# The start of an AdaLN block reordered between its engines, values in fours for two more half periods, and h of the second batch loaded in halves

## The chip, the cores and the metric

One core of a Trainium2 chip. The metric is the device time of one execution in microseconds, the median of several runs. The profiled execution is a single one of them; its times are counted from the start of its span.

## What is computed

A transformer block with adaptive layer norm, for two batches of 1024 rows of 1024 (fp32). Cut to what matters:

```python
mod = (silu(c) @ wmod).reshape(2, 6, 1, 1024)         # shift and scale a, gate a, shift and scale b, gate b
h = layernorm(x) * (1 + ca) + sa
q, k, v = h @ wq, h @ wk, h @ wv                      # 32 heads of 32; q and k are rotated (rope)
a = softmax(causal(q k^T / sqrt(32))) v
x = x + ga * (a @ wo)
h = layernorm(x) * (1 + cb) + sb
x = x + gb * ffn(h)     # h @ W_base^T + b_base, plus 8 gated low-rank experts (A_w, B_w, W_gate, W_thr)
```

## The kernel before

Every fp32 product is made as three products of rounded parts: hi*hi, lo*hi, hi*lo. ScalarE rounds a tile to its hi part, VectorE or GpSimd subtract for the rest (lo). Each engine runs an instruction order written out by hand; semaphores join them. All waits of SyncE's list, which issues nearly all DMAs, are in order too: an issue that waits holds up those behind it.

**The start.** Eight tiles of x (128 rows each) of batch 0 are loaded, normalised on VectorE (`ln_stats`, `ln_norm`; the root is GpSimd's `ln_rstd`), transposed on TensorE (`ln_turn`) and copied to xT (`ln_out`, half on VectorE, half on ScalarE). In the loop of VectorE, tile i-1 is normalised behind the statistics of tile i. wmod comes in 12 chunks of 2 MiB through four buffers; `mod_chunk(k)` multiplies chunk k on TensorE, `mod_out(k)` copies it out on ScalarE, `mod_cols(k)` turns it to columns. After chunk 3 `mod_vectors(0)` gives scale_a and shift_a. Then `ln_mod(c, kt)` scales the 128x512 piece (column block c, chunk kt) of xT on VectorE, `ln_round` rounds it on ScalarE, `ln_rest` subtracts, even kt on VectorE, odd kt on GpSimd. `chain(t, n, m0, m1)` is the projection of head group t: 24 products of 512 columns, n = 0 to 3 for q and k in both column blocks, 4 and 5 for v. Chains (0,0) and (0,2) follow the pieces one by one. Each q or k chain goes through rope: `rope_products` (VectorE), `rope_total` (GpSimd), `round_rot` (ScalarE), `rest_rot` (GpSimd, rot_lo), each waiting for the one before it through one buffer; when rot_lo is 2, then 4, SyncE copies the parts to stk (`stack`). `split_qk`/`rest_qk` and `split_v`/`rest_v` part the weights. `first_rows` then runs the first score rows, with the last wmod chunks and the chains of FIRST_CHAINS between them; wmod's chunks 8 to 11 are issued around the two stacks.

**The half periods.** 32 half periods u (PAIRS), each for two heads and 12 units i of scores; u = 2t and 2t+1 belong to head group t, and batch 1 begins with t = 8. In each unit TensorE has scores, row products for the next half period, a quarter of a chain and values. `PV_AT` sets after which units values are made: every second one, in FOURS every fourth, with six probs buffers instead of four; the last of FOURS has one group more, at unit 10. The two more buffers are x_next and h_pair, which also take wo's rows 0 and 1 at the end. Meanwhile batch 1's h is made and stored to HBM; at u = 13 `load_next_hT(c)` brings it into hT_lo (SyncE's queue) and hT_hi (ScalarE's queue) over batch 0's, block by block, once the last chain that reads the block is done.

**The end of it.** In u = 28 wo is loaded (`load_wo`), in 29 and 30 GpSimd parts it (`split_wo`), and `project` multiplies with it. a_raw and ga lie over buffers of the first phase. **Phase B** goes over 16 tiles; per tile TensorE multiplies h2 (made in two halves: `modulate_half` on VectorE, `split_h` on ScalarE and GpSimd) with wb. Its body waits for both halves, and for y_ev, VectorE's copy of the tile before out of ps_s.

## Time and profile before

| | |
|---|---|
| median of three runs | 1649.58 us (1647.54 to 1650.38) |
| the profiled execution | 1646.6 us, its span 1644.5 us |
| busy: TensorE, VectorE, ScalarE, GpSimd | 1569.2 (95%), 964.9 (59%), 1024.1 (62%), 616.9 (38%) us |
| mean granted TensorE clock | 0.98 of full |
| share of the chain that ended last | TensorE 79%, VectorE 6%, ScalarE 5%, DMA 4% |
| first scores (end of the start) | 138.23 us |

A busy share near 100% says that an engine has no room; the few per cent that are left stand in a few places, which only the timelines show. The granted clock of 1.0 is 2.4 GHz and 0.5 is 1.2 GHz. A line of a timeline can hold several like instructions (x4).

### The profile page before, as it was taken

The numbers are of one execution on the slowest core, as the hardware profiler recorded it, in microseconds if no ns is written. First come the engines' busy times: TensorE is split into PE (matmuls) and PEld (weight loads), VectorE is DVE, ScalarE is ACT, GpSimd is POOL, SyncE is SP. The second block draws the span as 40 slices with busy tenths as digits, with TensorE's granted clock in tenths as the row PEclk, the third lists the DMA queues.
The fourth block names the chain that finished last, engine by engine and source line by source line (L and its number), as shares of the span: only waits on it lengthen the run. The fifth ranks groups of instructions, "written<-read, shape, count | busy, mean of one in ns | idle before, by whom it ended". The sixth has DMA issues, their size and how long they took to land.

```text
span 1644.5 us, 29435 instructions
## 1 busy us (share of the span) xinstructions
PE 1569.2 (95%) x9530; PEld 1187.6 (72%) x9530; DVE 964.9 (59%) x2932; ACT 1024.1 (62%) x2662; POOL 616.9 (38%) x485
## 2 busy tenths in 40 slices
PE   5889999999999989999999999998989999999996
PEld 2556767667677767777777777775668888888885
DVE  5627577677765756566657567565653535353533
ACT  2337888989889978899899899888520101010100
POOL 3533253443534424234234244237114343333332
PEclk9999999999999999999999999996989999999998
DMA  9673444445443384333333333354332121212110
GB/s 350 229 256 82 108 99 126 110 110 146 113 123 79 81 270 98 76 92 77 92 80 87 91 75 82 86 156 135 84 98 72 43 76 39 77 40 77 38 64 26
DMA packets 172035, 174.43 MB, mean 106 GB/s; under 512 B 21045, under 2 KB 120677, under 8 KB 171897
## 3 DMA queue, kind: packets, MB, share of 16 engines
q1 hardware_dynamic: 169784, 168.54, 36.5%
q10 hardware_dynamic: 2112, 4.19, 0.8%
q8 instruction: 68, 1.11, 0.3%
q14 instruction: 71, 0.57, 0.1%
HBM read 96.65 MB, written 25.18 MB: 74 GB/s over the span
## 4 chain that ended last, share of the span: by engine, by line
PE 79%; DVE 6%; ACT 5%; issue 4%; DMA 4%; POOL 1%; SPq 1%; ACTq 0%; DVEq 0%
PE ps_s L1272 13%; PE ps_qkv L1272 13%; PE ps_s L719 11%; PE ps_pv L1341 9%; PE ps_s L1314 8%; PE ps_t L1283 7%; PE ps_qkv L691 5%; PE ps_s L691 5%; PE ps_s L721 1%; ACT probsT L1568 1%; ACT rows_sb L1532 1%; DMA x_start<-in_L_attn_x_dram 1%; DVE rows_sb L1799 1%; PE ps_s L1185 1%; PE ps_t L704 1%
## 5 line engine op out<-in xcount | busy, mean ns | idle before, releaser
L1532 ACT ACTIVATE rows_sb<-rows_sb,bias_m 128x640 f32<-128x640 f32 (+7 forms) x512 | 396.1, 774 | 12.5
L1799 DVE CUSTOM_DVE_ANT_0 rows_sb<-ps_t,mask 128x512 f32<-128x512 f32 (+3 forms) x512 | 296.8, 586 | 168.9 <-PE ps_t L1283 156.4
L1283 PE MATMUL ps_t<-stk 96*128 96x512 f32 (+3 forms) x768 | 268.9, 352 | 10.5 <-DVE smax L1799 7.0
L1568 ACT ACTIVATE probsT<-ps_s 128x512 f32<-128x512 f32 (+1 forms) x504 | 251.8, 537 | 33.6 <-PE ps_s L1314 17.2
L1314 PE MATMUL ps_s<-stk 98*128 98x512 f32 (+3 forms) x768 | 224.8, 374 | 3.2 <-DMA stk<-m_rows 2.0
L1825 DVE TENSOR_TENSOR ps_s<-ps_s,mask_t 128x128 f32<-128x128 f32 (+1 forms) x384 | 120.5, 340 | 158.8 <-PE ps_s L1314 155.5
L1283 PEld LDWEIGHTS ps_t<-stk 96*128 96x128 f32 x768 | 146.5, 191 | 58.8 <-DVE smax L1799 12.2
L1314 PEld LDWEIGHTS ps_s<-stk 98*128 98x128 f32 x768 | 132.4, 192 | 71.8 <-issue 34.3
L1960 POOL TENSOR_TENSOR rope_b<-rope_b,rope_sin 128x512 f32<-128x512 f32 x64 | 82.9, 1295 | 263.0 <-DVE rope_b L1784 263.0
L1272 PE MATMUL ps_qkv<-hT_hi,w_hi 128*128 128x512 f32 x384 | 158.6, 413 | 7.8 <-DVE hT_lo L1759 3.8
L1799 DVE CUSTOM_DVE_ANT_0 rows_sb<-ps_t,mask,smax_part 128x128 f32<-128x128 f32 (+3 forms) x256 | 140.7, 550 | 41.5 <-PE ps_t L1283 13.9
L1936 POOL TENSOR_TENSOR w_lo<-w_raw,w_hi 128x512 fp32r<-128x512 f32 x64 | 84.2, 1318 | 206.4 <-ACT w_hi L1480 206.4
L764 ACT ACTIVATE gsm<-ag_out,bthr 128x1 f32<-128x1 f32 x16 | 4.7, 294 | 248.2 <-DVE ag_out L851 248.2
L1272 PE MATMUL ps_s<-hT_hi,w_hi 128*128 128x512 f32 x384 | 155.9, 406 | 1.6 <-DVE rope_b L1784 1.5
L1272 PE MATMUL ps_qkv<-hT_lo,w_hi 128*128 128x512 f32 x384 | 152.3, 397 | 0.0
L1272 PE MATMUL ps_qkv<-hT_hi,w_lo 128*128 128x512 f32 x384 | 152.2, 396 | 0.0
L1272 PE MATMUL ps_s<-hT_lo,w_hi 128*128 128x512 f32 x384 | 151.4, 394 | 0.0
L1272 PE MATMUL ps_s<-hT_hi,w_lo 128*128 128x512 f32 x384 | 151.0, 393 | 0.0
L1341 PE MATMUL ps_pv<-probsT,v_all 128*32 128x128 f32 (+1 forms) x2272 | 146.0, 348 | 0.0
L1968 POOL TENSOR_TENSOR rot<-rope_b,rot 128x512 fp32r<-128x512 f32 x64 | 84.6, 1321 | 97.4 <-ACT rot L1502 97.4
L719 PE MATMUL ps_s<-wb_hi,h_hi 128*128 128x512 f32 x256 | 109.1, 426 | 7.1 <-POOL h_lo L922 5.1
L1341 PEld LDWEIGHTS ps_pv<-probsT,v_all 128*32 128x32 f32 x2272 | 70.8, 111 | 58.9 <-issue 23.9
(219 smaller groups left out, 3174.6 us busy)
## 6 DMA issues: line engine op xcount, KB each, us to landing
stk<-rot SPq DMA_DIRECT2D x384, 128.0 KB, 2.4
probsT<-in_L_wmod_dram SPq DMA_DIRECT2D x5, 2048.0 KB, 10.3
wm_one<-in_L_wmod_dram SPq DMA_DIRECT2D x5, 2048.0 KB, 14.2
w_raw<-in_L_attn_wq_dram SPq DMA_DIRECT2D x16, 512.0 KB, 4.0
w_raw<-in_L_attn_wk_dram SPq DMA_DIRECT2D x16, 512.0 KB, 4.7
w_raw<-in_L_attn_wv_dram SPq DMA_DIRECT2D x16, 512.0 KB, 4.1
attn_scratch<-attn_sb SPq DMA_DIRECT2D x128, 64.0 KB, 2.8
h_scratch<-h_pair SPq DMA_DIRECT2D x32, 256.0 KB, 2.9
```

The source lines that it names most:

```text
L691: mm = pe.matmul(q_bank[c], (a_hi, a_hi, a_lo)[way][:, kt, :], (wo_hi, wo_lo, wo_hi)[way][:, kt, c * BANK:(c + 1) * BANK], start=m % (3 * ...
L719: pe.matmul(ps_s[0][:, cols], h, w[:, kt, cols], start=(kt == 0 and n == 0), stop=False)
L1272: mm = pe.matmul(q_bank[(6 * t + n) % 2], w[:, j, kt, :], h[:, kt, cols], start=(m == 0), stop=(m == 3 * KT - 1))
L1283: pe.matmul(bank[:, 0:c1 - c0], stk[0:3 * HD, u % 2, 0, qt // 4, h, qt % 4 * P:(qt % 4 + 1) * P], stk[0:3 * HD, u % 2, 1, part, h, 0:c1 - ...
L1314: mm = pe.matmul(s_bank[w % 3][:, a * n:(a + 1) * n], stk[0:3 * HD + 2, u % 2, 1, kt // 4, h, kt % 4 * P:(kt % 4 + 1) * P], stk[0:3 * HD + ...
L1341: mm = pe.matmul(ps_pv[to:to + HD, first // 2 * P:BANK // 2], v_all[:, t % 2, kt, at:at + HD], tiles[:, first - at0:4 - at0:2, :], start=k ...
L1532: act.activation(row, row, ACT.Exp, bias=bias_m[:, qt, h:h + 1], scale=SCALE, accum_out=sums[:, qt // 4, h, qt % 4:qt % 4 + 1]).then_inc(s ...
L1568: act.activation(probs[PROBS[w]][:, hs[0]:hs[-1] + 1, 0:n], s_bank[(NS * u + k) % 3][:, 0:len(hs) * n].rearrange("p (h n) -> p h n", h=len ...
L1799: dve.tensor_tensor_reduce(rows_sb[:, to, at + c0:at + c1], bank[:, 0:n], mask[:, BANK - n:BANK] if last else mask[:, 0:1].broadcast_to([P ...
L1825: dve.tensor_tensor(part, part, mask_t[:, :].unsqueeze(1).broadcast_to([P, len(hs), P]), ALU.add).then_inc(tri_ok, 1)
L1936: pool.tensor_tensor(w_lo[:, j, ks, :].rearrange("p k (h e m) -> p (k h) e m", h=GH, e=2), w_raw[:, (3 * t + j) % 2, ks, :].rearrange("p k ...
L1968: pool.tensor_tensor(rot[:, j, 1, cols].bitcast(F32R), rope_b[:, :], rot[:, j, 0, cols], ALU.subtract).then_inc(rot_lo, 1)
```

## The change

- x of tiles 6 and 7 is loaded behind wmod's chunk 3 and wk's first group; VectorE's first loop runs over six tiles. Tiles 6 and 7 are normalised, turned and copied after column block 0 is scaled; their turns stand on TensorE behind mod 4 and within chain (0,1), in banks of their own.
- Of each pair of pieces VectorE scales the even one, ScalarE the odd one (an Identity activation), and VectorE makes both rests. GpSimd makes none, and does wk's rests ahead of them and the first two rope turns right behind each other. The order of mod_out, split and round_rot on ScalarE is changed to go with it.
- h of batch 1 is loaded in halves of four chunks; the first half of block 0 as soon as chain (7,4) is half through (half_mm).
- FOURS goes to 29. wo's rows 0 and 1 go to rope_cos and rope_sin, loaded later in u = 28; load_a(0) waits for the first wo rest, load_ga no longer waits for one.
- Phase B's products wait for each half of h2 at its first chunk.

The diff, cut (declarations of semaphores, store_next's count, and places where only names change are left out; ScalarE's load_next_hT has the same new waits as SyncE's):

```diff
-FOURS = range(11, PAIRS - 4)
+FOURS = range(11, PAIRS - 2)
...
-        wo_raw = [x_next[:, :], h_pair[:, :, :].rearrange("p a n -> p (a n)")]
+        wo_raw = [rope_cos[:, :], rope_sin[:, :]]
...
         def load_ga(sp):
 
-            sp.wait_ge(wo_lo_ok, 2)
             sp.wait_ge(gate_st, 16)
...
                 i = tile_of(hp, e)
-                pe.wait_ge(h2_hi_ok, 2 * i + 2)
-                pe.wait_ge(h2_lo_ok, 2 * i + 2)
                 pe.wait_ge(ag_cp, i + 1)
                 pe.wait_ge(y_ev, i + 1)
                 for c in range(0, D, BANK):
                     for kt in range(KT):
+                        if c == 0 and kt % 4 == 0:
+                            pe.wait_ge(h2_hi_ok, 2 * i + kt // 4 + 1)
+                            pe.wait_ge(h2_lo_ok, 2 * i + kt // 4 + 1)
...
-        ln_bank = [[s_bank[2], s_bank[1]], q_bank]
+        ln_bank = [[s_bank[2], s_bank[1]], q_bank] * 3 + [[s_bank[2], s_bank[1]]] * 2
...
             load_wmod(2)
             load_w(0, 0)
+            load_wmod(3)
+            load_w(1, 0)
             load_x(6)
             load_x(7)
-            load_wmod(3)
-            load_w(1, 0)
             load_wmod(4)
...
-            def load_next_hT(c):
+            def load_next_hT(c, half):
 
                 sp.wait_ge(h_st, 2 * 16 * 2 * NT)
-                sp.wait_ge(proj_mm, 6 * G - 1 + c)
-                for half in range(2):
-                    sp.dma_start(hT_lo[:, 4 * half:4 * half + 4, c * BANK:(c + 1) * BANK].bitcast(F32), h_dram[1].rearrange(
...
+                if half:
+                    sp.wait_ge(proj_mm, 6 * G - 1 + c)
+                else:
+                    sp.wait_ge(half_mm, c + 1)
+                sp.dma_start(hT_lo[:, 4 * half:4 * half + 4, c * BANK:(c + 1) * BANK].bitcast(F32), h_dram[1].rearrange(
...
                 if u == 2 * G - 3:
-                    load_next_hT(0)
+                    load_next_hT(0, 1)
...
-                if u == PAIRS - 4:
-                    sp.wait_ge(ln_tr, 4 * NT)
-                    for k in range(2):
-                        load_wo(k)
...
                 if u == 2 * G - 3:
-                    load_next_hT(1)
+                    for half in range(2):
+                        load_next_hT(1, half)
                 if u == PAIRS - 3:
-                    sp.wait_ge(rope_mul, 4 * T)
+                    sp.wait_ge(wo_lo_ok, 1)
                     load_a(sp, 0)
...
                 if u == PAIRS - 4:
-                    sp.wait_ge(proj_mm, 6 * (T - 1) + 4)
-                    for k in range(4, KT):
+                    sp.wait_ge(rope_mul, 4 * T)
+                    sp.wait_ge(rope_sin_ok, 4 * T)
+                    for k in (0, 1, *range(4, KT)):
                         load_wo(k)
                 store_attn(2 * u)
...
+                if u == 2 * G - 4:
+                    load_next_hT(0, 0)
...
                     if t == 0 and n in (0, 2) and way == 0:
                         pe.wait_ge(ln_hi, KT * c + kt + 1)
-                        if kt % 2:
-                            pe.wait_ge(ln_lo, KT // 2 * c + kt // 2 + 1)
-                        else:
-                            pe.wait_ge(ln_lo_even, KT // 2 * c + kt // 2 + 1)
+                        pe.wait_ge(first_lo, KT * c + kt + 1)
...
+                    if t == G - 1 and n >= 4 and m == 3 * KT // 2 - 1:
+                        mm.then_inc(half_mm, 1)
...
             for k in range(FIRST_MOD):
-                ln_turn(2 * k)
-                ln_turn(2 * k + 1)
+                if k < 3:
+                    ln_turn(2 * k)
+                    ln_turn(2 * k + 1)
                 mod_chunk(k)
...
             for n in range(4):
-                chain(0, n, 0, 3 * KT)
+                chain(0, n, 0, 6)
+                if n == 1:
+                    ln_turn(7)
+                chain(0, n, 6, 3 * KT)
                 if n:
                     mod_cols(FIRST_MOD + n - 1)
                 mod_chunk(FIRST_MOD + n)
+                if n == 0:
+                    ln_turn(6)
...
+            def ln_mod(c, kt):
+
+                if kt == 1:
+                    act.wait_ge(mcol, 1)
+                    for half in range(2):
+                        act.wait_ge(ln_tt[half], 4 * (c + 1))
+                part = xT[:, kt, c * BANK:(c + 1) * BANK]
+                act.activation(part, part, ACT.Identity, bias=shift_a[:, B * kt:B * kt + 1],
+                               scale=scale_a[:, B * kt:B * kt + 1]).then_inc(h_odd, 1)
+
             def ln_round(c, kt):
-                act.wait_ge(h_ok, KT * c + kt + 1)
+                act.wait_ge(h_odd if kt % 2 else h_even, KT // 2 * c + kt // 2 + 1)
...
-            for kt in range(KT):
-                ln_round(0, kt)
             for n in range(2, 4):
                 split_qk(0, n)
-            mod_out(4)
-            for kt in range(KT):
-                ln_round(1, kt)
-            mod_out(5)
+            for c in range(2):
+                for kt in range(0, KT, 2):
+                    ln_mod(c, kt + 1)
+                    ln_round(c, kt)
+                    ln_round(c, kt + 1)
+                if c == 0:
+                    mod_out(4)
+                    ln_out(6)
+                    ln_out(7)
+            round_rot(0, 0)
             for half in range(2):
                 split_v(0, half)
-            round_rot(0, 0)
+            mod_out(5)
             round_rot(0, 1)
-            mod_out(6)
             for n in range(2):
                 split_qk(1, n)
+            mod_out(6)
+            round_rot(0, 2)
             mod_out(7)
-            round_rot(0, 2)
             round_rot(0, 3)
...
-                    if u == 2 * G - 3 and i in (0, 4):
-                        load_next_hT(i // 4)
+                    if (u, i) == (2 * G - 4, NU - 2):
+                        load_next_hT(0, 0)
+                    if (u, i) == (2 * G - 3, 0):
+                        load_next_hT(0, 1)
+                    if (u, i) == (2 * G - 3, 4):
+                        for half in range(2):
+                            load_next_hT(1, half)
...
-            for i in range(NT + 2):
-                if i < NT:
+            for i in range(6 + 2):
+                if i < 6:
                     ln_stats(0, i)
-                if 0 < i <= NT:
+                if 0 < i <= 6:
                     ln_norm(0, i - 1)
...
             for c in range(2):
-                for kt in range(KT):
-                    ln_mod(c, kt)
-                    if kt % 2:
-                        ln_rest(c, kt - 1)
-                    if (c, kt) == (1, 4):
+                ln_mod(c, 0)
+                for kt in range(0, KT, 2):
+                    if kt + 2 < KT:
+                        ln_mod(c, kt + 2)
+                    ln_rest(c, kt)
+                    ln_rest(c, kt + 1)
+                    if (c, kt) == (1, 2):
                         rope_products(0, 0)
+                if c == 0:
+                    for tt in (6, 7):
+                        ln_stats(0, tt)
+                    for tt in (6, 7):
+                        ln_norm(0, tt)
+                    for tt in (6, 7):
+                        ln_out(tt)
             rope_products(0, 1)
...
-            def ln_rest(c, kt):
-                pool.wait_ge(ln_hi, KT * c + kt + 1)
...
-            for i in range(2, NT):
+            for i in range(2, 6):
+                ln_rstd(0, i)
+            for n in range(4):
+                rest_qk(0, n)
+            for i in (6, 7):
                 ln_rstd(0, i)
             for n in range(2):
-                rest_qk(0, n)
-            for kt in range(1, KT, 2):
-                ln_rest(0, kt)
-            for n in range(2, 4):
-                rest_qk(0, n)
-            for kt in range(1, KT, 2):
-                ln_rest(1, kt)
-                if kt == 3:
-                    rope_total(0, 0)
+                rope_total(0, n)
+                rest_rot(0, n)
             for half in range(2):
                 rest_v(0, half)
-            rest_rot(0, 0)
-            rope_total(0, 1)
-            rest_rot(0, 1)
             for n in range(2):
                 rest_qk(1, n)
```

## Rows read from the trace of the kernel before

**Rows 1.** Chain that ended last, 0 to 130 us: start us, length us, what
```profile
24.36 8.97 DMA x_start<-in_L_attn_x_dram
...
103.77 12.01 DMA probsT<-in_L_wmod_dram
```

**Rows 2.** Windows: stretch us, length, busy per engine (instructions), PE clock, DMA share, GB/s
```profile
20.00:40.00 20.00, 15.47 (x104) 7.43 (x96) 12.88 (x23) 6.12 (x11) 5.95 (x10) 0.92 1.05 381
...
40.00:60.00 20.00, 15.53 (x88) 9.87 (x88) 13.37 (x18) 9.14 (x16) 8.82 (x7) 0.91 0.72 250
```

**Rows 3.** Timeline of TensorE, 15 to 160 us: start, length, engine, line, operation [idle <-releaser]
```profile
43.04 1.92 PE L1185 MATMUL ps_s<-wm_more,v_all 128*32 128x512 f32 x16
...
59.87 1.92 PE L1185 MATMUL ps_s<-probsT,v_all 128*32 128x512 f32 x16
...
67.45 0.95 PE L1196 MATMUL ps_pv<-sel,x_next 128*128 128x2 f32 x8
...
77.15 0.95 PE L1196 MATMUL ps_pv<-sel,x_next 128*128 128x2 f32 x8
...
98.40 3.48 PE L1185 MATMUL ps_s<-probsT,v_all 128*32 128x512 f32 x16 [3.06 <-DMA probsT<-in_L_wmod_dram]
...
121.99 1.92 PE L1185 MATMUL ps_s<-wm_one,v_all 128*32 128x512 f32 x16
...
138.23 0.72 PE L1314 MATMUL ps_s<-stk 98*128 98x512 f32 x2
```

**Rows 4.** Timeline of SyncE's DMA queue, 0 to 150 us
```profile
86.24 3.99 SPq L1033 DMA_DIRECT2D stk<-rot  x6
```

**Rows 5.** Timeline of VectorE, 0 to 140 us
```profile
47.34 1.00 DVE L1753 TENSOR_SCALAR xT<-xT,scale_a,shift_a 128x512 f32<-128x512 f32 x2 [0.21 <-DVE scale_a L1708]
...
48.57 0.69 DVE L1759 TENSOR_TENSOR hT_lo<-xT,hT_hi 128x512 fp32r<-128x512 f32 x1 [0.23 <-ACT hT_hi L1460]
...
49.18 1.97 DVE L1753 TENSOR_SCALAR xT<-xT,scale_a,shift_a 128x512 f32<-128x512 f32 x2
...
52.00 1.96 DVE L1753 TENSOR_SCALAR xT<-xT,scale_a,shift_a 128x512 f32<-128x512 f32 x2
```

**Rows 6.** Timeline of ScalarE, 0 to 140 us
```profile
47.92 1.14 ACT L1460 CAST hT_hi<-xT 128x512 fp32r<-128x512 f32 x2 [2.31 <-DVE xT L1753]
...
114.14 0.72 ACT L1532 ACTIVATE rows_sb<-rows_sb,bias_m 128x512 f32<-128x512 f32 x1
```

**Rows 7.** Timeline of GpSimd, 0 to 140 us
```profile
49.14 1.28 POOL L1924 TENSOR_TENSOR hT_lo<-xT,hT_hi 128x512 fp32r<-128x512 f32 x1 [2.22 <-ACT hT_hi L1460]
```

**Rows 8.** Timeline of TensorE: the m transposes at the starts of half periods 10, 11, 13, 14
```profile
487.67 0.27 PE L1289 MATMUL ps_t<-ident,m_col 128*8 128x128 f32 x1
...
519.84 0.27 PE L1289 MATMUL ps_t<-ident,m_col 128*8 128x128 f32 x1
...
582.28 0.27 PE L1289 MATMUL ps_t<-ident,m_col 128*8 128x128 f32 x1
...
622.80 0.27 PE L1289 MATMUL ps_t<-ident,m_col 128*8 128x128 f32 x1
```

**Rows 9.** Timeline of TensorE in half period 13, 570 to 626 us
```profile
592.70 0.88 PE L1314 MATMUL ps_s<-stk 98*128 98x512 f32 x2 [1.98 <-DMA stk<-m_rows]
...
596.70 0.77 PE L1272 MATMUL ps_qkv<-hT_hi,w_hi 128*128 128x512 f32 x1 [2.70 <-DMA hT_lo<-h_scratch]
```

**Rows 10.** Timeline of SyncE's DMA queue, 570 to 630 us
```profile
586.63 0.95 SPq L1093 DMA_DIRECT2D hT_lo<-h_scratch  x2
```

**Rows 11.** Window of 3 us in half period 29, columns as in rows 2
```profile
1116.00:1119.00 3.00, 3.00 (x20) 1.51 (x20) 0.64 (x3) 2.66 (x9) 2.92 (x2) 0.54 0.00 0
```

**Rows 12.** Timelines of GpSimd, VectorE and TensorE at phase B's last tile
```profile
1612.64 1.26 POOL L922 TENSOR_TENSOR h_lo<-h2t,h_hi 128x512 fp32r<-128x512 f32 x1 [7.60 <-ACT h_hi L754]
...
1615.32 1.22 DVE L885 TENSOR_TENSOR xn<-ps_s,bias 128x1024 f32<-128x1024 f32 x1
...
1617.50 0.76 PE L719 MATMUL ps_s<-wb_hi,h_hi 128*128 128x512 f32 x1 [5.10 <-POOL h_lo L922]
```

More of the change, by code:

```diff
@@ L1004, in store_next @@
             def store_next(tt, half):
-                sp.wait_ge(ln_lo, NT + 2 * tt + half + 1)
+                sp.wait_ge(ln_lo, 2 * tt + half + 1)
                 for a, part in enumerate((h_next_hi, h_next)):
@@ L1248, in chain @@
                         for half in range(2):
-                            pe.wait_ge(ln_tt[half], NT)
+                            pe.wait_ge(ln_tt[half], 6)
                     if n < 2 and t:
@@ L1753, in ln_mod @@
                 dve.tensor_scalar(part, part, scale_a[:, B * kt:B * kt + 1], shift_a[:, B * kt:B * kt + 1], ALU.mult,
[L1754 removed]
+                                  ALU.add).then_inc(h_even, 1)
             def ln_rest(c, kt):
```

39 lines of the change are left out of this document (20 added, 19 removed).

## The prediction

> **What bounds the kernel now.** I read the page first: TensorE is busy 95% of the span of 1644.5 us (the table above). So time can only come from stretches in which TensorE idles, runs at the lower granted clock, or does avoidable work. The windows, the chain of waits and the times of one transpose that occurs twice in each half period then show where these are. There are four.
>
> (a) The start, up to the first scores at 138.23. The chain runs through loads of x and wmod and through short hand-overs between engines [rows 1 to 7].
> (b) Half period 13, where batch 1's h replaces batch 0's in SBUF. From 582.28 to 622.80 is 40.52 us; the two half periods before it take 62.44 together, 31.22 each [rows 8]. TensorE idles 1.98 us for the m rows and 2.70 us for hT_lo [rows 9].
> (c) Half periods 28 and 29, where values go in groups of two units and TensorE falls to the lower clock.
> (d) The last tile of phase B, 5.10 us of idle before its product [rows 12].
> Elsewhere TensorE has no gap, and the change adds it no work there. The profiled execution took 1646.6 us, 3.0 below the median of 1649.6. I sum changes and put them on the median.
>
> **Part 1, the start.** Four steps.
>
> *The x order.* Tile 5 is normalised after tile 6's statistics, and x of tile 6 landed at 24.36+8.97=33.33 [rows 1]. The new loops take six tiles first, so tiles 4 and 5 flow at once, and the wait is for wmod's fourth chunk. Loads land in order at 381 GB/s, 0.363 MiB per us [rows 2]. By size, x6 was at 10.64 MiB of the stream; the fourth chunk now ends at 12.14. It lands at 33.3+1.5/0.363=37.5. Its products start there instead of at 43.04 [rows 3]: ahead of them turn 5 runs behind turn 4 (to about 34), mod 2 takes 1.92 and mod_cols 0.9, to 36.8. Vectors follow as before, so the first scaling starts at 47.34-5.4=41.9 [rows 5].
>
> *Scaling.* Before, a pair of chunks takes 2.81 us (49.18 to 52.00). Two DVE scalings alone take 1.00 together; beside a POOL rest of 1.28 the two take 1.97 [rows 5, 7]. So DVE's scaling stands while POOL's subtraction runs. After, DVE scales one of a pair and makes both rests (the next instruction starts 0.61 behind a rest), 0.50+2x0.61=1.7 [rows 5]; ACT scales one and rounds two. Two rounds take 1.14, and the nearest row for scaling with a bias column, an exp of 128x512, takes 0.72 [rows 6], so ACT needs 1.65 to 1.85. I take 1.75 a pair, and 1 us more once, because POOL's w_lo for wk now runs beside the first pair. The last chunk is ready at 41.9+2.3+3x1.75+0.6=50.0, and chain (0,0) ends at 50.9 where it ended at 59.87 [rows 3]. So far 9.0.
>
> The Trainium skill, "SBUF — State Buffer", section "SBUF: two separate sides", calls the pair of ports that DVE and GpSimd share an exclusive lock: one blocks for the other's whole instruction. By that rule the 1.97 is one scaling held back, as in the trace, and the rests moved to DVE, with two SBUF inputs, can be blocked too where rope_total on POOL runs beside them. That would add up to 1.3 us twice in the second column block, which TensorE does not reach before.
>
> *Tiles 6 and 7.* They are now normalised behind the first block. DVE's queue holds two statistics, two norms and copies: 50.0 to 57.7; ACT's last copy is at 58.0. TensorE meanwhile has mod 4 (to 52.8), turn 6 (waits to 54.0), the first six products of chain (0,1), turn 7 and the rest; a product starts every 0.23 us ((67.45-61.8)/24) [rows 3]. It finishes chain (0,1), mod_cols and mod 5 at 64.3. The second block runs 58.1 to about 67.5 with rope_products(0,0) inside, one chunk ahead of TensorE, so chain (0,2) ends at 69.8. It ended at 77.15 [rows 3]; the gain is 7.4, and the waits at turn 6 and 7 (1.5) are what it lost. Cover for late x is about 2 us; beyond it each us costs one.
>
> *Rope and rows.* rope_total(0,0) no longer queues behind four rests on POOL, so rot_lo reaches 2 at 74.7, and the stack starts there, not at 86.24 [rows 4]. rest_v and rest_qk(1,*) now stand between the second and third rope turn, 5 us of POOL: rot_lo is 4 at 90.6. wmod's chunk 8 lands near 87 where TensorE took it at 98.40, after 3.06 of idle and at the lower clock (3.48 against 1.92) [rows 3]. ACT's mod_out(7) now stands behind round_rot(0,2): about 1 us. Chunk 10 is issued behind the second stack, 94.9; it took 12.01 from its issue before [rows 1], so it lands between 102.5 (bandwidth alone) and 107; TensorE wants it at 102.2. I take a wait of 2. From chunk 11's products the tail is unchanged, 138.23-121.99=16.2 [rows 3], from 110.2: first scores at 126.4. **Gain 11.8**, bounds 8 and 14. Later half periods have no slack that swallows it.
>
> **Part 2, batch 1's h.** The first halves of block 0 (2 MiB in hi and lo) are issued once chain (7,4) is half through, some 5 us ahead of 582.28, at about 577; SP issued hT_lo at 586.63 [rows 10]. They land by 583.5 (2 MiB at 0.363, and 1 us). The second halves follow at 582 and 586.6 and land near 593, and chunk 4 is wanted two units after chunk 0, at about 596. The m rows (wanted at 592.70-1.98=590.7) sit behind 1.85 MB instead of 3, 4.9 us at 381 GB/s from 583.5, so they land between 588.5 and 590. So both waits and the clock drop behind them go, and the half period takes 31.3 to 32.4 instead of 40.5. Issues on ACT and SP are equally many; SP's first one now waits behind store_attn, and behind it stands only the next stack, which waits for the last scores of 12 anyway. **Gain 8.1**, bounds 5 and 9.2 (block 1's lo halves still go ahead of a stack).
>
> **Part 3, fours to 29.** Half period 10, in twos, takes 519.84-487.67=32.17, and 11 and 12, in fours, 31.22 [rows 8]: 0.95 for three groups fewer, 0.32 a group. Extended, 27 has one group fewer, 28 three, 29 two: 6x0.32=1.9. In 29 TensorE is at 1.2 GHz (granted 0.54 in the window from 1116, the lower level behind the idle before it) [rows 11], and the flush puts two more units there, so I take **1.5**, bounds 0 and 3. wo rows 0 and 1 go to rope_cos and rope_sin, loaded last in 28: six issues wait about 1.3 us longer for POOL's sine product and push the next stack by 1 us; POOL takes the first only when 29's chain is done, 8 us into 29, which hides both; uncovered it would be 1 us. load_a's new wait ends before its turn; dropped waits are free.
>
> **Part 4, phase B.** TensorE may start a tile on half of h2. On 15 tiles nothing waited. On the last, POOL's first half ends at 1612.64+1.26=1613.90, and the product began at 1617.50, after the second [rows 12]. Yet it also waits for y_ev, DVE's copy at 1615.32 lasting 1.22, that is 1616.54 [rows 12]. So not 3.6 but **0.9**; what is late next is that copy, which stands behind modulate on DVE.
>
> **Sum.** 11.8+8.1+1.5+0.9=22.3, and 1649.6-22.3=1627.3 us.
>
> **Rivals.** *R1, half of the start's gain is swallowed.* The second stack and chunks 10 and 11 of wmod collide, or late x holds up the second block, so that the scores come at 132: total 16 to 17, 1633. For it: the 12.01 us of chunk 10. Against: its queue is emptier at 95 than at 103. Chance 0.16.
> *R2, the swap still stalls.* Part 2 gives 2 because m rows and stack wait behind the earlier halves: 1633.4. For: TensorE's 1.98 wait for m rows. Against: less is queued. Chance 0.08.
> *R3, more goes.* In 29 nearly 30 us run at 1.2 GHz. If six probs buffers keep the clock up, some 4 us go too, and the start gives 14: 1621. Chance 0.12.
> *R4, slower.* Between 42 and 126 TensorE waits for each chunk of h with two thirds of a microsecond of work in 1.75. If the clock stays at 1.2 GHz there, the 65 us of full-clock products up to the scores double. It decides from 22 us of them on, a third of the stretch; at half of it the time is 1649.6-22.3+33=1660. For: mod 8 behind 3.06 of idle ran at 3.48 [rows 3]. Against: in the window from 40 to 60, where TensorE also waited for chunks, the granted clock was 0.91 [rows 2]. Chance 0.04. The Trainium skill, "TensorE: Matmul & The Clock Gate", section "What's actually happening", says that the default state is throttled and activity releases it. By that rule R4 needs gaps to go on, and from 51 the plan has few.
> *R5, nothing.* The new gates do not bind as said (the halves still land late and x7 holds up all): 1648. Chance 0.03.
>
> **Numbers.** Forecast 0.57, its own range 1623 to 1631.5; R1 to R5 take 0.43. The range reaches to R1, R2 and most of R3: 1619 to 1637. Faster by over 0.2% (3.3 us, about what a measurement of this kernel can tell from no change): 0.92; same 0.04; slower 0.04.
>
> **What would show it.** First scores near 126; scaling pairs 1.7 us apart; chain (0,2) from 64; half period 13 near 32 us with no DMA wait; 28 near 31.3; last product about 0.9 earlier against y_ev. Wrong would be a wait on turn 6 or 7 above 3 us, scores after 130, or half period 13 above 35.

## The result and the profile after

The change makes the kernel faster by about 1%. In the same session the kernel before took 1647.54 us (median of 5 runs) and the changed one 1630.6 us (1627.56 to 1633.2, 5 runs): a ratio of 0.9897, 95% interval 0.988 to 0.9914, 16.9 us less. The forecast was 1627.3, the range 1619 to 1637.

| | before | after | forecast |
|---|---|---|---|
| median, us | 1647.54 | 1630.6 | 1627.3 |
| span of the profiled execution | 1644.5 | 1631.4 | |
| first scores | 138.23 | 129.51 | 126.4 |
| half period 13 | 40.52 | 38.80 | 31.3 to 32.4 |
| half periods 27 to 29 together | 98.91 | 96.50 | 1.5 less |
| idle before the last tile's product | 5.10 | 4.22 | 0.9 less |

The half periods are read off as in [rows 8]. The profiled execution of the changed kernel took 1633.2 us, the longest of its five runs, which matters for half period 13 below.

**The start.** TensorE's timeline of the changed kernel, columns as in [rows 3]: chunk 3's products, the first product of chain (0,0), mod 4 behind that chain, the wait for chain (0,2)'s last piece, mod_cols behind that chain, the columns of the last vectors of the second block, chunk 10, the first scores.

```profile
38.76 1.92 PE L1190 MATMUL ps_s<-wm_more,v_all 128*32 128x512 f32 x16 [1.83 <-DMA wm_more<-in_L_wmod_dram]
...
45.78 0.77 PE L1274 MATMUL ps_qkv<-hT_hi,w_hi 128*128 128x512 f32 x1 [3.23 <-DVE hT_lo L1791]
...
53.68 1.92 PE L1190 MATMUL ps_s<-probsT,v_all 128*32 128x512 f32 x16
...
71.61 0.47 PE L1274 MATMUL ps_qkv<-hT_hi,w_hi 128*128 128x512 f32 x1 [0.70 <-DVE hT_lo L1791]
...
72.38 0.95 PE L1201 MATMUL ps_pv<-sel,x_next 128*128 128x2 f32 x8
...
86.27 1.05 PE L1201 MATMUL ps_pv<-sel,x_next 128*128 128x2 f32 x8 [0.72 <-ACT x_next L1459]
...
107.12 1.92 PE L1190 MATMUL ps_s<-probsT,v_all 128*32 128x512 f32 x16 [2.29 <-DMA probsT<-in_L_wmod_dram]
...
129.51 0.72 PE L1318 MATMUL ps_s<-stk 98*128 98x512 f32 x2
```

Where [rows 3] had 43.04, 59.87, 77.15 and 138.23, this has 38.76, 53.68, 72.38 and 129.51. The gain is 4.3, 6.2, 4.8 and 8.7 us. VectorE's timeline beside the two scaled blocks (the first scalings and four rests of the first block, then the same of the second):

```profile
43.06 1.98 DVE L1785 TENSOR_SCALAR xT<-xT,scale_a,shift_a 128x512 f32<-128x512 f32 x2 [0.21 <-DVE scale_a L1740]
...
48.28 2.54 DVE L1791 TENSOR_TENSOR hT_lo<-xT,hT_hi 128x512 fp32r<-128x512 f32 x4
...
59.63 1.00 DVE L1785 TENSOR_SCALAR xT<-xT,scale_a,shift_a 128x512 f32<-128x512 f32 x2 [0.44 <-ACT xT L1464]
...
65.65 5.81 DVE L1791 TENSOR_TENSOR hT_lo<-xT,hT_hi 128x512 fp32r<-128x512 f32 x4
```

ScalarE's timeline, its scalings of the first block:

```profile
42.94 0.81 ACT L1474 ACTIVATE xT<-xT,shift_a,scale_a 128x512 f32<-128x512 f32 x1 [0.51 <-DVEq L1741]
...
44.69 0.81 ACT L1474 ACTIVATE xT<-xT,shift_a,scale_a 128x512 f32<-128x512 f32 x1
```

GpSimd's timeline, the first turn of rope:

```profile
65.39 1.50 POOL L1995 TENSOR_TENSOR rope_b<-rope_b,rope_sin 128x512 f32<-128x512 f32 x1 [10.13 <-DVE rope_b L1816]
66.97 1.63 POOL L1997 TENSOR_TENSOR rope_b<-rope_a,rope_b 128x512 f32<-128x512 f32 x1
...
69.33 1.58 POOL L2003 TENSOR_TENSOR rot<-rope_b,rot 128x512 fp32r<-128x512 f32 x1 [0.73 <-ACT rot L1522]
```

ScalarE's pairs stand 1.75 us apart (42.94, 44.69). Four rests take 2.54 us while GpSimd is idle, and 5.81 beside its rope. SyncE's DMA queue, the two stacks and the issue of chunk 10, which answers to [rows 4]:

```profile
77.53 3.97 SPq L1036 DMA_DIRECT2D stk<-rot  x6
...
93.30 3.80 SPq L1036 DMA_DIRECT2D stk<-rot  x6
97.14 0.59 SPq L990 DMA_DIRECT2D probsT<-in_L_wmod_dram  x1
```

Windows of 2 us over chain (0,0), with the columns of [rows 2] (a count takes in an instruction that only reaches into the window):

```profile
44.00:46.00 2.00, 0.22 (x1) 0.25 (x2) 2.00 (x3) 2.00 (x5) 0.75 (x1) 0.50 1.06 391
46.00:48.00 2.00, 2.00 (x5) 1.57 (x6) 2.00 (x5) 2.00 (x5) 0.00 (x0) 0.50 1.05 384
48.00:50.00 2.00, 2.00 (x6) 1.56 (x5) 2.00 (x4) 2.00 (x4) 0.00 (x0) 0.50 1.03 380
50.00:52.00 2.00, 2.00 (x8) 1.55 (x8) 2.00 (x4) 0.02 (x1) 0.00 (x0) 0.85 1.05 380
```

Behind 3.23 us of idle the granted clock is 0.50, the lower level of 1.2 GHz. TensorE counts as busy throughout, but from 46 to 50 only 9 products start, one every 0.43 us, where the full rate, one every 0.23 us, is 17.

**Half period 13.** One window from m transpose to m transpose, same columns, of the kernel before:

```profile
582.28:622.80 40.52, 34.72 (x219) 25.58 (x218) 19.11 (x69) 29.71 (x78) 6.37 (x5) 0.92 0.97 294
```

And of the changed kernel:

```profile
573.43:612.23 38.80, 34.29 (x220) 25.43 (x218) 19.07 (x69) 29.56 (x78) 6.37 (x5) 0.96 0.93 275
```

TensorE's idle in it goes from 5.80 us to 4.51. The 5.80 are the two waits of [rows 9] and a third, at the end of the half period, which TensorE's timeline of the kernel before has here:

```profile
620.98 0.30 PE L1283 MATMUL ps_t<-stk 96*128 96x128 f32 x1 [1.12 <-DMA stk<-rot]
```

Both waits that are left are for stk. TensorE's timeline of the changed kernel:

```profile
585.09 0.73 PE L1318 MATMUL ps_s<-stk 98*128 98x512 f32 x2 [3.21 <-DMA stk<-m_rows]
...
610.41 0.30 PE L1287 MATMUL ps_t<-stk 96*128 96x128 f32 x1 [1.30 <-DMA stk<-rot]
```

SyncE's DMA queue around the m rows:

```profile
567.87 0.37 SPq L1098 DMA_DIRECT2D hT_lo<-h_scratch  x1
...
576.25 1.41 SPq L1043 DMA_DIRECT2D stk<-m_rows  x2
```

The DMA view of the changed kernel, 568 to 588 us:

```profile
DMA packets 4569, 6.02 MB, mean 301 GB/s; under 512 B 265, under 2 KB 2099, under 8 KB 4567
```

The first half is issued 5.6 us ahead of the half period's start at 573.43, and the wait of 2.70 for hT_lo [rows 9] is gone. The m rows, though, are wanted at 581.88 and land at 585, 3.21 late where they were 1.98 late before.

**The end.** TensorE's timeline at the last tile, which answers to [rows 12]:

```profile
1604.60 0.76 PE L722 MATMUL ps_s<-wb_hi,h_hi 128*128 128x512 f32 x1 [4.22 <-DVE xn L888]
```

VectorE's timeline there:

```profile
1603.28 1.21 DVE L888 TENSOR_TENSOR xn<-ps_s,bias 128x1024 f32<-128x1024 f32 x1
```

The releaser is now VectorE's copy of y, as the prediction named it, 0.88 us earlier.

### The profile page after: what moved, and what is told of

Its sections match the earlier page's. It is cut to its first block, busy times and chain, and to the rows that moved or that the text cites. A ratio compares the mean times of both kernels' runs of the same rounds, so it can differ in the third digit from the quotient of the medians.

```text
span 1631.4 us, 29469 instructions
## 1 busy us (share of the span) xinstructions
PE 1561.2 (96%) x9530; PEld 1189.2 (73%) x9530; DVE 962.8 (59%) x2932; ACT 1026.9 (63%) x2670; POOL 605.7 (37%) x477
## 4 chain that ended last, share of the span: by engine, by line
PE 76%; DVE 6%; DMA 5%; ACT 5%; issue 4%; POOL 2%; SPq 1%; ACTq 0%; DVEq 0%; POOLq 0%
PE ps_qkv L1274 13%; PE ps_s L1274 13%; PE ps_s L722 10%; PE ps_pv L1345 8%; PE ps_s L1318 8%; PE ps_t L1287 7%; PE ps_qkv L693 5%; PE ps_s L693 5%; ACT probsT L1588 1%; PE ps_s L724 1%; ACT rows_sb L1552 1%; DVE rows_sb L1831 1%; DMA wm_more<-in_L_wmod_dram 1%; DVE h_pair L1800 1%; PE ps_t L706 1%
## 5 line engine op out<-in xcount | busy, mean ns | idle before, releaser
L1588 ACT ACTIVATE probsT<-ps_s 128x512 f32<-128x512 f32 (+1 forms) x488 | 243.1, 536 | 34.3 <-PE ps_s L1318 18.2
L1345 PE MATMUL ps_pv<-probsT,v_all 128*32 128x256 f32 (+1 forms) x2208 | 139.9, 343 | 0.0
```

The lines of the kernel that those rows point to most:

```text
L1345: mm = pe.matmul(ps_pv[to:to + HD, first // 2 * P:BANK // 2], v_all[:, t % 2, kt, at:at + HD], tiles[:, first - at0:4 - at0:2, :], start=k ...
L1588: act.activation(probs[PROBS[w]][:, hs[0]:hs[-1] + 1, 0:n], s_bank[(NS * u + k) % 3][:, 0:len(hs) * n].rearrange("p (h n) -> p h n", h=len ...
```

## The experiments

Spans, half periods and gaps are those of each kernel's one profiled execution; "the tail" is from the last m transpose, at the end of half period 30, to the end of the span (476.63 us before, 476.77 after). The expectation of the last run names that point the end of half period 31.

**1. again.** The changed kernel, unedited.

> The changed kernel, unchanged, for a second profile. In the first one the two traces stand 13.1 us apart (1644.5 to 1631.4), the medians 16.9. Theory A (the profiled execution was a slow one of its kind, and the difference lies where DMA decides): this profile's span is 1626 to 1630, and against the first it is shorter at half period 13 or at the start, all half periods between alike. Theory B (the difference is in the kernel before, whose profiled run was 1 us below its median): the span is again 1631 and half period 13 again 38.8.

1629.3 us, ratio 0.9904 (0.9885 to 0.9924), in a session in which the kernel before took 1645.83. Up to half period 13 nothing moves (the first m transpose stands at 117.68, in the first profile at 117.50), but half period 13 takes 35.50 instead of 38.80. TensorE's timeline:

```profile
583.82 0.73 PE L1318 MATMUL ps_s<-stk 98*128 98x512 f32 x2 [1.60 <-DMA stk<-m_rows]
```

And the window:

```profile
573.76:609.26 35.50, 32.74 (x219) 24.71 (x218) 19.10 (x69) 29.47 (x78) 6.35 (x5) 1.00 0.99 296
```

The same program waits 1.60 or 3.21 us for the same transfer, and in the first profile the clock drops besides (0.96), which costs 1.55 more (34.29 against 32.74 busy). The floor of this half period is those 32.74: in it TensorE has 219 instructions.

Six more profiles, of kernels described below that load h in the same way (halves_only, copy_first, rope_behind, scale_one, x_early and both), fill the space between: the m rows are waited for 1.60 to 2.66 us and the half period takes 35.44 to 37.51. They also show that the length of that wait doesn't decide the clock. TensorE's timeline and the window of half period 13 of copy_first:

```profile
584.51 0.74 PE L1319 MATMUL ps_s<-stk 98*128 98x512 f32 x2 [2.66 <-DMA stk<-m_rows]
...
573.40:609.98 36.58, 32.79 (x219) 24.63 (x218) 19.12 (x69) 29.56 (x78) 6.36 (x5) 1.00 0.99 290
```

And of scale_one:

```profile
589.11 0.74 PE L1318 MATMUL ps_s<-stk 98*128 98x512 f32 x2 [1.80 <-DMA stk<-m_rows]
...
578.87:616.35 37.48, 34.29 (x219) 25.48 (x218) 19.10 (x69) 29.48 (x78) 6.35 (x5) 0.95 0.94 284
```

A wait of 2.66 leaves the clock at 1.00, one of 1.80 comes with 0.95.

**2 to 4. One part alone.** Each is the kernel before with one part of the change: start_only has the new start; halves_only loads h in halves (core of the edit below); fours_only has FOURS to 29 and wo's new places. The per-half waits of phase B are in none of the three.

```diff
-                sp.wait_ge(proj_mm, 6 * G - 1 + c)
...
+                if half:
+                    sp.wait_ge(proj_mm, 6 * G - 1 + c)
+                else:
+                    sp.wait_ge(half_mm, c + 1)
```

> Of the change, only the start (x order, scaling by two engines, rests on VectorE, the orders that go with it); h of batch 1, fours, wo and phase B as before. If the parts add up: 8.7 us less than before, first scores at 129.5, half period 13 at 40.5 us. If the start helps the swap too (other phase of the DMA queues): over 10 less.

> Of the change, only batch 1's h in halves. By the trace of the changed kernel it gives 1.8 us (40.5 to 38.8 in half period 13, the wait for hT_lo gone, the wait for the m rows grown from 1.98 to 3.2). By my prediction it gives 8.1; for that the m rows would have to land by 590.7. If the halves are worth more alone than with the rest, 4 or more.

> Of the change, only fours to 29 and wo's rows 0 and 1 in rope_cos and rope_sin. Groups alone at 0.32 us each: 1.9 less. The trace of the changed kernel shows 2.5 between half periods 27 and 31. Rival: wo's later loads cost some of it where the rest of the change does not cover them: 0 to 1.

| | median | ratio (interval) | less than before | what moved in the trace |
|---|---|---|---|---|
| start_only | 1638.96 | 0.9956 (0.9941 to 0.997) | 6.9 | first scores 132.10 |
| halves_only | 1641.75 | 0.9976 (0.9965 to 0.9987) | 4.1 | half period 13 at 35.55 |
| fours_only | 1644.4 | 0.9993 (0.9983 to 1.0003) | 1.4 | half periods 27 to 29 at 96.55 |

Together 12.4 where the whole change gives 16.5 in that session. Of the 4.1 missing, 0.9 is phase B's: in all three the last tile's product still waits 5.08 us. The larger part stands in one place of start_only's profile, chunk 3's products,

```profile
38.98 3.14 PE L1188 MATMUL ps_s<-wm_more,v_all 128*32 128x512 f32 x16 [1.67 <-DMA wm_more<-in_L_wmod_dram]
42.05 3.58 PE L1199 MATMUL ps_pv<-sel,x_next 128*128 128x2 f32 x16
```

take 3.14 and the columns 3.58, where after had 1.92 and 1.95 behind a wait that was as long (1.83). That is the lower clock, and chain (0,0) ends 2.5 us later (56.20 against 53.68). It is no mark of this kernel: of the others with the same start, hi_later, scale_one and both had it too, and wv_later ran these products at full clock behind a shorter wait:

```profile
38.85 1.92 PE L1192 MATMUL ps_s<-wm_more,v_all 128*32 128x512 f32 x16 [1.26 <-DMA wm_more<-in_L_wmod_dram]
```

The rest of the 4.1 is within what the intervals leave open (each reaches 1.6 to 3.2 us either way); nothing shows that the parts depend on each other. fours_only isn't told from no change by its time; the half periods show 2.36 us less, the same as in the whole change.

**5 and 6. Who is ahead of the m rows.** hi_later issues ScalarE's second half of block 0 two units later; m_first puts SyncE's m rows ahead of their stack.

```diff
-                    if (u, i) == (2 * G - 3, 0):
+                    if (u, i) == (2 * G - 3, 2):
                         load_next_hT(0, 1)
```

```diff
+                if u == 2 * G - 3:
+                    place_m(u, 1)
                 if u + 1 < PAIRS:
                     sp.wait_ge(st_ok, NS * u)
...
-                place_m(u, 1)
+                if u != 2 * G - 3:
+                    place_m(u, 1)
```

> The changed kernel, with ScalarE's issue of the second half of hT_hi (block 0) two units later, behind unit 2 of half period 13 instead of unit 0. Theory Q (the m rows wait because 1 MiB of hT_hi, issued 2 to 3 us ahead of them, is carried with them at only 250 to 300 GB/s): the wait for the m rows falls from 1.6 to 3.2 to under 0.5, the clock stays up, half period 13 takes 32.5 to 33.5 instead of 35.5 to 38.8, the time is 2 to 4 lower, and the half lands before chunk 4 of chain (8,0). Rival L (the latency of the m rows' own DMA and the stack ahead of them decide): the wait stays above 1.

> The changed kernel, with the m rows of half period 13 issued ahead of the stack of 14 instead of behind it (on SyncE's queue, some 2 us earlier and with 0.8 MB less ahead). Theory Q (bytes queued ahead decide, whoever issued them): 0.8 MB at 270 GB/s is 3 us, so the wait for the m rows is gone, half period 13 takes about 32.5 and the time is 2 to 4 lower. Rival H (what is ahead in ScalarE's hT_hi decides alone): the wait falls by the 2 us of earlier issue at most and the hT_hi half still holds it: half period 13 34 to 36.

hi_later 1628.64, ratio 0.9895 (0.9878 to 0.9911); m_first 1630.13, 0.9902 (0.9886 to 0.9919): neither differs from the changed kernel. The wait for the m rows is gone in both, and others stand in its place. TensorE's timeline of hi_later:

```profile
609.00 0.44 PE L1287 MATMUL ps_t<-stk 96*128 96x128 f32 x1 [2.68 <-DMA stk<-rot]
```

And of m_first:

```profile
583.87 0.47 PE L1290 MATMUL ps_t<-stk 96*128 96x512 f32 x1 [1.41 <-DMA stk<-rot]
...
608.55 0.30 PE L1290 MATMUL ps_t<-stk 96*128 96x128 f32 x1 [2.70 <-DMA stk<-rot]
```

Half period 13 is 36.85 and 36.81, where 32.5 to 33.5 was expected: a longer wait at its end takes what the start of it gave back, and in hi_later the granted clock of the half period is 0.96 besides.

**7. wv_later.** wv's load is issued behind the attention stores.

```diff
-                if p and t + 2 < T:
+                if p and t + 2 < T and u != 2 * G - 3:
                     load_w(2, t + 2)
...
+                if u == 2 * G - 3:
+                    load_w(2, t + 2)
```

> The changed kernel, with wv's group (0.5 MiB in 512-byte rows) loaded in the second half of half period 13 instead of its first. Theory S (the DMA engines are busy from 570 to 588 with some 6 MB at 301 GB/s, and TensorE waits for whatever comes last of it; putting one transfer ahead only moved the wait from the m rows to the stack): 0.5 MB less in the stretch is 1.7 us less waiting, half period 13 takes 33.5 to 35, the time is 1 to 2.5 lower than the changed kernel. Rival L (one transfer's own latency): no change, 35.5 to 38.8.

1632.12, ratio 0.9917 (0.9894 to 0.9941). The m rows' wait is 1.54, the stack's 0.98, half period 13 takes 35.23; again had 1.60, 1.16 and 35.50. The edit tests little: the load stood behind the m rows already, it is now issued at 581.82, 3.8 us behind them instead of 2.0 (again), and the DMA engines are still full (the DMA view of 568 to 588 us):

```profile
DMA packets 5174, 6.29 MB, mean 314 GB/s; under 512 B 265, under 2 KB 2731, under 8 KB 5172
```

That the half period is held by how much has to move in it, and not by one place in a queue, fits the runs 5 to 7. It isn't shown: none of them took bytes out of the half period.

**8. copy_first.** In phase B, VectorE evicts y between the two halves of modulate, since TensorE's first product waits for that copy and the first half only.

```diff
-                    modulate(i + 1, bj)
+                    modulate_half(i + 1, bj, 0)
...
                     dve.tensor_tensor(xn[:, :], ps_s[0][:, :], bias[:, :], ALU.add).then_inc(y_ev, 1)
+                    modulate_half(i + 1, bj, 1)
```

> The changed kernel, with VectorE's copy of y (which gives y_ev) ahead of the second half of modulate instead of behind it. If y_ev is what the last tile's first product waits for since the change (4.22 us, on VectorE xn): it starts once the first half of h_lo is done, 2.7 us earlier, and with less idle before it the clock comes back sooner: the stretch from the last transpose of m to the end is 3 to 5 shorter than 476.2. If the second half of h2 is then late instead: under 1.5 shorter.

1621.6 us in a single execution, beside 1645.12 for the kernel before; no interval. TensorE's timeline:

```profile
1595.74 0.47 PE L722 MATMUL ps_s<-wb_hi,h_hi 128*128 128x512 f32 x1 [1.64 <-POOL h_lo L926]
```

The wait is 1.64 instead of 4.22 and its releaser is GpSimd's first half. The tail is 469.27, 7 us shorter, more than the 2.6 of the wait; run 12 asks for the difference.

**9. rope_behind.** GpSimd starts rope only when all rests are made.

```diff
             for i in (6, 7):
                 ln_rstd(0, i)
+            pool.wait_ge(first_lo, 2 * KT)
             for n in range(2):
                 rope_total(0, n)
```

> The changed kernel, with GpSimd's first rope turn held until VectorE has made the last rest of block 1, so that no GpSimd instruction runs beside the rests. In the changed kernel the last four rests of block 1 take 5.81 us beside GpSimd's rope instructions, those of block 0 2.54 with GpSimd idle. If one engine holds the other up (Trainium skill, SBUF - State Buffer: an exclusive lock on the shared port pair): the four rests take 2.5, chain (0,2) ends 0.7 earlier, and the rope chain starts later by less than it was held, within 2 us: first scores within 1.5 us either way. If VectorE waited for ScalarE's rounding instead: the four rests keep 5 or more.

1632.55 in one execution. VectorE's timeline:

```profile
67.15 2.50 DVE L1791 TENSOR_TENSOR hT_lo<-xT,hT_hi 128x512 fp32r<-128x512 f32 x4
```

TensorE's:

```profile
110.23 3.32 PE L1190 MATMUL ps_s<-probsT,v_all 128*32 128x512 f32 x16 [2.20 <-DMA probsT<-in_L_wmod_dram]
```

The same four rests, alone, take 2.50 instead of 5.81: the two engines hold each other up. Yet GpSimd's first sine product starts at 69.73 instead of 65.39, and the first stack is issued at 80.62 instead of 77.53, 3.1 later. Of that 1.5 was there before the edit acts (chain (0,0) ends at 55.18 instead of 53.68), so waiting loses 1.6 us. The scores start at 135.71, 6.2 later, but most of that isn't the edit's either: besides the 1.5, chunk 10's products run at the lower clock (3.32 against 1.92), and the stretch from the first m transpose to the next takes 17.43 instead of 15.91 (granted 0.57 from 124 to 128; wv_later has 17.46 there, by the clock too). Rope beside the rests, slow as both are, is the better order, by 1.6 us.

**10. scale_one.** VectorE scales both pieces of a pair; x stays late.

```diff
-                    ln_mod(c, kt + 1)
...
-                                  ALU.add).then_inc(h_even, 1)
+                                  ALU.add).then_inc(h_odd if kt % 2 else h_even, 1)
...
+                ln_mod(c, 1)
...
+                        ln_mod(c, kt + 3)
```

> The changed kernel, with all pieces scaled by VectorE (ScalarE scales none); the rests stay on VectorE. By counting instructions VectorE needs 2x0.50+2x0.61=2.2 us a pair instead of ScalarE's 1.75: chain (0,0) ends 1.5 to 2 later than 53.7, first scores 1 to 2 later than 129.5. If splitting the scaling matters more (VectorE then waits for ScalarE's rounds in turn): 3 or more. If it is hidden: under 0.5.

1637.01 in one execution. Chain (0,0) ends at 57.29 instead of 53.68 and the scores start at 134.76 instead of 129.51. TensorE's timeline:

```profile
39.79 3.02 PE L1190 MATMUL ps_s<-wm_more,v_all 128*32 128x512 f32 x16 [0.99 <-DMA wm_more<-in_L_wmod_dram]
...
57.29 1.92 PE L1190 MATMUL ps_s<-probsT,v_all 128*32 128x512 f32 x16
```

Chunk 3's products begin 1.0 later here and, with their columns, take 2.7 longer at the lower clock (3.02 and 3.58 against 1.92 and 1.95), so the first scaling starts 3.8 later, at 46.82. Chain (0,0) ends 3.6 later, no more: there ScalarE's share of the scaling gives nothing, since TensorE at the lower clock is what the chain waits for. At the scores 5.2 are missing, 1.5 more than the late first scaling brings, and that is what the split is worth, as far as one profile tells.

**11. x_early.** x of tiles 6 and 7 is loaded and normalised as in the kernel before, everything else as changed.

```diff
+            load_x(6)
+            load_x(7)
             load_wmod(3)
             load_w(1, 0)
-            load_x(6)
-            load_x(7)
...
-            for i in range(6 + 2):
-                if i < 6:
+            for i in range(NT + 2):
+                if i < NT:
```

> The changed kernel, with x of tiles 6 and 7 back ahead of wmod's fourth chunk and normalised, turned and copied in the first loops. By the trace the order of x gave 4.3 us at wmod's fourth chunk (43.04 to 38.76); the late tiles cost about 1 us in chain (0,1). If both hold to the end: first scores 3 to 4 later than 129.5. If a later wait (wmod's chunk 10, or the rope chain) is what decides: under 1.5.

1635.48 in one execution. Chunk 3's products at 42.99 and chain (0,0) to 58.82; scores at 132.47. TensorE's timeline:

```profile
108.65 1.92 PE L1190 MATMUL ps_s<-probsT,v_all 128*32 128x512 f32 x16 [1.92 <-DMA probsT<-in_L_wmod_dram]
```

The order of x is worth 5.1 us at chain (0,0) and 1.5 at chunk 10. At the scores it looks like 3.0, but 1.4 of these arise behind the first m transpose, where the granted clock falls (0.58 from 121 to 125, behind a wait of 0.89; after has 1.00 behind 0.90) and the next transpose comes 17.34 us later instead of 15.91. So about 1.6 of the start's 8.7 us is the order of x. The rest, about 7, is the scaling split, 1.5 by run 10, and GpSimd's shorter queue ahead of rope, to which I put the larger part. No run has the queue's order alone; what speaks for it is the stack: here the first stack is issued at 79.15, 7.1 ahead of 86.24 [rows 4], though chain (0,0) ends only 1.05 ahead of 59.87 [rows 3].

**12. both.** copy_first, and mod_out(7) ahead of a rounding of rope on ScalarE.

```diff
+            mod_out(7)
             round_rot(0, 2)
-            mod_out(7)
```

> The changed kernel with two moves at once, neither of which leaves work out: the last tile's residual y is evicted behind its normalisation copies (as in the run copy_first), and the scaled columns of the last tile of the first batch are made on ScalarE ahead of a rounding of the rope (0.7 us less wait was seen ahead of mod_cols(7) in the changed kernel). If the end was held by the clock and the wait ahead of the last tile's first product, the tail (from the end of half period 31) is 469.3 again, 7 us under the changed kernel's 476.2 to 476.8, and the time is 1621 to 1623, ratio to the kernel before 0.985 to 0.987. If copy_first's single look was a lucky draw of the clock, the tail is 474 to 477 and the time 1628 to 1630. For the second move: if chunk 10 of wmod is what the last products wait for, the 0.7 us is swallowed by the wait for that transfer and the first scores stay at 129.5; if the columns were on the path, they start at 128.8.

1628.14 us (1626.69 to 1628.42, 4 runs) beside 1645.1: ratio 0.9891, interval 0.9871 to 0.9911. TensorE's timeline:

```profile
38.76 3.47 PE L1191 MATMUL ps_s<-wm_more,v_all 128*32 128x512 f32 x16 [1.05 <-DMA wm_more<-in_L_wmod_dram]
...
109.20 1.92 PE L1191 MATMUL ps_s<-probsT,v_all 128*32 128x512 f32 x16 [2.25 <-DMA probsT<-in_L_wmod_dram]
...
1600.97 0.47 PE L722 MATMUL ps_s<-wb_hi,h_hi 128*128 128x512 f32 x1 [1.65 <-POOL h_lo L926]
```

The wait of 0.72 before the columns is gone (87.45), and swallowed: chunk 10 is used 10.0 us after its issue at 99.22, as after has it (97.14 to 107.12). The scores come at 131.60, since chunk 3's products fell to the lower clock. The wait at the last tile is 1.65 again, so that part of copy_first is real. The tail is 473.45: neither 469.3 nor 476. The window of the last tile, from its first product to the end of the span, of the changed kernel:

```profile
1604.60:1631.40 26.80, 18.55 (x79) 15.03 (x79) 6.78 (x18) 0.85 (x4) 8.29 (x5) 0.82 0.10 40
```

Of copy_first:

```profile
1595.74:1619.80 24.06, 15.80 (x79) 12.77 (x79) 8.15 (x22) 1.47 (x5) 8.85 (x5) 0.95 0.11 44
```

Of both:

```profile
1600.97:1626.60 25.63, 17.40 (x79) 14.07 (x79) 8.14 (x22) 1.47 (x5) 8.83 (x5) 0.86 0.10 42
```

The same 79 instructions take 18.55, 15.80 or 17.40 us by the clock alone. copy_first had the best of these, and its stretch from the end of half period 30 to the last tile's wait was 2.6 us shorter than both's, though the two kernels are the same there. Without the edit 17.40 occurs too: wv_later, behind its wait of 4.22, has it and a tail of 473.9, and the unedited tails run from 473.9 to 478.4 (m_first). TensorE's timeline of wv_later, where the first product runs at full clock (0.47) behind the wait behind which after had 0.76:

```profile
1600.24 0.47 PE L722 MATMUL ps_s<-wb_hi,h_hi 128*128 128x512 f32 x1 [4.22 <-DVE xn L888]
```

So the 1621.6 was a lucky single execution; the edit takes 2.6 us of wait away, and the timed runs of both kernels cannot tell whether the median moved (0.9891 against 0.9904, intervals that overlap).

## Why the prediction was right, and where its steps were off

The time lay in the range, 3.3 us above the forecast; by differences 16.9 came where 22.3 was forecast, 5.4 less. The 2.0 between the two is luck: the kernel before had 1649.58 as the median of its first three runs and 1647.54 with two more. The bottlenecks were the four named, and three of the four changes acted as described. The sizes were off in two terms, and by the prediction's own signs one thing was wrong: half period 13 stayed above 35 in every profile.

**The start: 8.7, forecast 11.8, inside its bounds of 8 and 14.** At chain (0,0) 2.8 us are missing already. Chain (0,0) was put at 50.9. Chunk 3's products began at 38.76, not 37.5, 1.3 late. ScalarE's scaling took 0.81, not 0.72, yet the pairs came 1.75 apart as forecast, and the last piece was ready at 50.82 against 50.0. The largest part, 2 us, is a step that the prediction left out: TensorE was taken to follow the pieces at once, 0.9 us behind the last, but it stood at the lower clock from 44 to past 50, so chain (0,0) had work left when the last piece came and ended 2.86 behind it. I had weighed this clock only as a rival over the whole start (R4), not for one chain. R4's row, 0.91 over 20 us [rows 2], was too coarse: cut into windows of 2 us the same trace has 0.60 and 0.55 from 50 to 54, and the changed kernel has 0.50 from 44 to 50. All other kernels with the new start have this too (their first product of the chain takes 0.76 or 0.77 us), but no run kept the clock up there, so the 2 us are read off the timeline, not tested. Half of that lateness was then made up: turn 6 didn't wait, the second block began at 59.63 against 58.1, and TensorE came to chain (0,2) at 65.60 against 64.3, 1.3 late. The chain itself then lost another 1.2 to held-up rests (next paragraph), and from there on each step kept its length: first stack 77.53 against 74.7, second 93.30 against 90.6, chunk 10 at 107.12 against 104.2, scores 3.1 late.

The second step that was off is this one. That rests beside rope can be blocked, the Trainium skill's lock on the ports that VectorE and GpSimd share ("SBUF — State Buffer", section "SBUF: two separate sides"), is borne out by experiment 9: 5.81 against 2.50. The prediction named it and put it at nothing, since TensorE would not reach these pieces before. It did reach them: in after it waits 0.70 us for the last one, and chain (0,2) takes 6.78 us (65.60 to 72.38) where rope_behind, with rests that nothing holds up, needs 5.6 (67.09 to about 72.7). That is 1.2 of the 2.6.

**The swap of h: 1.7 in the first profile, 5.0 in again, 5.0 alone in halves_only, 3.0 to 5.1 in five more; forecast 8.1, bounds 5 and 9.2.** The first half did come 5.6 us ahead and the wait for hT_lo is gone, as forecast. What failed is the step by which the m rows sit behind 1.85 MB, moved at 381 GB/s, and land between 588.5 and 590. In the 20 us around it 6.02 MB moved, at 301 GB/s (319 in again). I had counted h and left out the stack, the stores and the weights that run beside it, and I took the rate of the start, 381, though the kernel before moved 323 GB/s here (582 to 602 us, with the DMA engines full). Then the wait varied from 1.60 to 3.21 between executions. And the end of the half period, a stack wait of 0.9 to 1.4 that the kernel before had too (1.12 at 620.98), had no row in my reading, which said that TensorE has no gap elsewhere. R2 named the right mechanism (the m rows wait behind the earlier halves) at a price of 2; the first profile is at that price, the other seven lie between it and the forecast. The forecast of 8.1 was out of reach from the start: TensorE has 32.74 us of work here, so that 7.8 was the most that could go.

**Fours: 2.4 over half periods 27 to 29, forecast 1.5, inside 0 to 3.** 27 gave 1.2, 28 0.9 and 29 0.3. The count of groups was right, 0.32 us a group too small in 27; why one group gave 1.2 there isn't shown.

**Phase B: 0.88 of wait, forecast 0.9.** The reading that the product also waits for y_ev is shown by the new releaser and by copy_first and both, in which the next one, GpSimd's first half, follows at 1.64. It cannot be seen in the tail (476.77 against 476.63), which varies by more than that between executions.

**Against the rivals.** R1 (scores at 132) did not come in the changed kernel: 129.51 and 129.70, and 129.4 to 129.6 in copy_first and m_first. Where the clock fell on the way, the scores did come at its time: 131.2 in hi_later and wv_later, 131.6 in both, 132.1 in start_only. R3 had half period 29 at the full clock; it fell by 0.3 only (33.18 to 32.84), and to 30.71 in one execution, m_first. Its premise, nearly 30 us at 1.2 GHz, was read off a window of 3 us and is wrong: the granted clock over the whole half period was 0.80 before, with 1.00 from 1100 to 1110, and it is 0.88 after. R4 and R5 didn't happen. By the medians the time lies between forecast and R1, for other reasons than R1's.

**What stays open.** What decides whether chunk 3's products, half period 13 and the last tile run at the lower clock was not found; no experiment aimed at it. Nor was what sets how long the m rows are waited for. That a version beats the changed kernel is not shown either.

## What to carry to other kernels

Before a transfer is moved earlier, add up all bytes of the stretch and divide by the rate that this mix reached there: with full DMA engines, letting the m rows go ahead of another transfer only moved the wait to a third, in two experiments. Read the granted clock in windows as short as the wait before them, and charge a chain that starts behind such a wait at the lower clock: chain (0,0) did so in every profile with the new start (2.58 to 3.79 us of idle), the last tile behind 4.22 us in most. Take the floor of a stretch from TensorE's busy time in it at full clock, not from its neighbours, and never trust one execution of a kernel whose executions differ by several microseconds.

## What the hardware showed beyond expectation

- **The clock draws differently for like waits.** 16 products of 512 columns took 1.92 us behind 1.83 us of idle (after), but also behind 1.26 (wv_later), 3.14 behind 1.67 (start_only), 3.02 behind 0.99 (scale_one) and 3.47 behind 1.05 (both). That the length of the idle time alone decides is ruled out by these rows. With the columns behind them the low draw costs 1.7 to 2.9 us. The Trainium skill, "TensorE: Matmul & The Clock Gate", section "What's actually happening", has the throttled state as the default; the rows agree insofar as chain (0,0) starts at 0.5 behind 3.23 us of idle, and the last tile does in most profiles (first product 0.76), though in wv_later it starts at full clock behind the same 4.22.
- **VectorE and GpSimd slow each other down.** Four subtractions of 128x512 on VectorE took 2.50 us alone and 5.81 beside GpSimd's three; GpSimd's own took 1.50, 1.63 and 1.58 where they take 1.29, 1.29 and 1.26 alone (rope_behind).
- **Full DMA engines moved 301 to 319 GB/s** in the swap (568 to 588 us in after and again, busy share 1.03), and 380 to 391 in the start (44 to 52 us, share 1.03 to 1.06).
